# Attention over edges and two norms on one core: all engines' steps in a new order, gathered rows transposed tile by tile, two closing jobs

## The reference

```python
q = (h @ Wq).reshape(n, H, DK); k = (h @ Wk).reshape(n, H, DK); v = (h @ Wv).reshape(n, H, DK)   # H 8, DK 64
e = einsum('ehd,ehd->eh', k[src], q[dst]) / sqrt(DK)
m = segment_max(e, dst, n); ex = exp(e - m[dst]); z = segment_sum(ex, dst, n); attn = ex / z[dst]
a = segment_sum(attn[:, :, None] * v[src], dst, n).reshape(n, DM)
x = _layernorm(h + a @ Wo, ln1_g, ln1_b)
f = relu(x @ W1 + b1) @ W2 + b2                      # 512 -> 64 -> 512
x = _layernorm(x + f, ln2_g, ln2_b)
out = _layernorm(h + x)                              # a last norm, without gain and bias
```

## Time and profile before

| | us |
|---|---|
| median of 3 runs | 683.0 (682.57 to 683.35) |
| span of the profiled execution | 682.0 |
| TensorE busy (matmuls) | 641.5 (94%) |
| TensorE weight loads, beside the matmuls | 483.8 (71%) |
| VectorE busy | 578.0 (85%) |
| ScalarE busy | 528.3 (77%) |
| GpSimd busy | 401.7 (59%) |
| granted TensorE clock, mean | 0.986 |
| HBM traffic over the span | 135 GB/s |

### The profile page before, as it was taken

How to read it: one execution, slowest core, us unless ns; L and a number is a source line. 1 busy time by engine, 2 the same in 40 slices (tenths; PEclk the granted TensorE clock), 3 DMA queues, 4 the chain that set the end, 5 groups by cost and what they waited for, 6 DMA issues and landing times. The chain is left out here.

```text
span 682.0 us, 10864 instructions
## 1 busy us (share of the span) xinstructions
PE 641.5 (94%) x3520; PEld 483.8 (71%) x3520; DVE 578.0 (85%) x1391; ACT 528.3 (77%) x1140; POOL 401.7 (59%) x363
## 2 busy tenths in 40 slices
PE   5999999999999999999999999999999999999950
PEld 2778877777777777777777777777778778675520
DVE  7668769879898898898889889988989898899792
ACT  2525269877888987988798889878878999698881
POOL 7267244867675865756776574864547726735423
PEclk9999999999999999999999999999999999999995
DMA  7844154644643745674474456455554824536452
GB/s 227 220 101 133 44 123 106 173 122 142 148 121 131 159 121 148 167 157 92 146 177 117 113 161 137 105 168 123 127 128 155 184 62 135 139 77 138 131 113 91
DMA packets 37747, 91.44 MB, mean 134 GB/s; under 512 B 8346, under 2 KB 9642, under 8 KB 37690
## 3 DMA queue, kind: packets, MB, share of 16 engines
q0 software_dynamic: 31536, 82.74, 47.6%
q1 hardware_dynamic: 6154, 8.01, 4.3%
HBM read 71.20 MB, written 20.99 MB: 135 GB/s over the span
## 5 line engine op out<-in xcount | busy, mean ns | idle before, releaser
L558 ACT ACTIVATE squares<-rows,nmean 125x512 bf16<-125x512 f32 x200 | 142.3, 713 | 41.5 <-DVE nmean L902 19.8
L412 POOL DMA_INDIRECT x_rows<-in_x_dram,node_idx x40 | 48.2, 1205 | 56.8 <-DVE rows L917 47.3
L416 POOL DMA_INDIRECT out_dram<-rows,node_idx x40 | 46.4, 1160 | 56.4 <-ACT rows L618 47.0
L473 POOL DMA_DIRECT2D x_rows<-in_L_gnn_ln_b_dram x40 | 52.9, 1372 | 31.1 <-DVE rows L821 21.7
L898 DVE SCALAR_TENSOR_TENSOR rows<-pF,rows 125x512 f32<-125x512 f32 x78 | 50.6, 686 | 23.2 <-PE pF L1103 22.5
L963 PE MATMUL pP<-wo_hi,aT_hi 128*125 128x512 f32 x160 | 65.9, 412 | 0.3 <-DVE aT_lo L848 0.3
L963 PE MATMUL pP<-xTs_hi,wv_hi 128*128 128x500 f32 x160 | 65.8, 411 | 0.0
L963 PE MATMUL pP<-xTd_hi,wq_hi 128*128 128x500 f32 x160 | 65.4, 409 | 0.1
L963 PE MATMUL pP<-xTs_hi,wk_hi 128*128 128x500 f32 x160 | 63.5, 397 | 0.6 <-ACT q L539 0.6
L963 PE MATMUL pP<-wo_lo,aT_hi 128*125 128x512 f32 x160 | 63.1, 394 | 0.0
L963 PE MATMUL pP<-wo_hi,aT_lo 128*125 128x512 f32 x160 | 63.0, 394 | 0.0
(11 more groups left out here) (197 smaller groups left out, 1760.6 us busy)
## 6 DMA issues: line engine op xcount, KB each, us to landing
x_rows<-in_L_gnn_ln_b_dram POOLq DMA_DIRECT2D x40, 512.0 KB, 6.7
dst_row<-in_dst_dram SPq DMA_DIRECT2D x9, 250.5 KB
q<-in_L_gnn_Wq_dram SPq DMA_DIRECT2D x1, 1024.0 KB, 5.6
rows<-in_L_gnn_Wk_dram SPq DMA_DIRECT2D x1, 1024.0 KB, 7.8
rows<-in_L_gnn_Wv_dram SPq DMA_DIRECT2D x1, 1024.0 KB, 6.8
x_rows<-in_L_gnn_Wo_dram SPq DMA_DIRECT2D x8, 128.0 KB, 6.0
xd<-in_x_dram,dst_idx POOLq DMA_INDIRECT x40, 4.6
xs<-in_x_dram,src_idx POOLq DMA_INDIRECT x40, 3.8
```

The lines of the kernel that those rows point to most:

```text
L412: pool.indirect_dma_start(rows, None, x, bass.IndirectOffsetOnAxis(ap=table[:, column:column + 1].bitcast(U32), axis=0), bounds_check=N - ...
L416: pool.indirect_dma_start(out, bass.IndirectOffsetOnAxis(ap=table[:, column:column + 1].bitcast(U32), axis=0), rows, None, bounds_check=N ...
L473: pool.dma_start(xr_wide[n], bass.AP(tensor=be2.tensor, offset=be2.offset, ap=[[0, P], [0, 2], [1, D]]), accum_op=ALU.add).then_inc(s[f"be ...
L558: ins = act.activation(squares[:, t, :], w[n][:, t, :], ACT.Square, bias=nmean[c][n][:, t:t + 1], accum_out=sq[c][n][:, t:t + 1])
```

## The change

**New order.** PLAN is replaced by one list per engine with a due number for each step of each round ("-" where a round lacks the step), and `sequence()` only sorts it. Nearly every engine's order is another one. The parts that the steps below speak of:

- TensorE, head. Before: ... COUNT0 COUNT1 TXD0 to TXD3 COUNT2 Q0 Q1 TXS0 TXS1 COUNT3 COUNT4 TXS2 Q2 TXS3 ROFF Q3 K0 FOLD K1 .... After: TURN1 TURN2 OFFS TURNF TXD0 FOLD TXD1 COUNT0 COUNT1 TXD2 TXD3 COUNT2 COUNT3 TXS0 Q0 TXS1 Q1 TXS2 TXS3 COUNT4 Q2 Q3 ROFF TXD0/1 (TXD0 of round 1) BITS K0 to K3 TXD1/1 TXD2/1 V0 S ....
- VectorE, head. After: CAST1 TABD CAST2 FLAG FILLI TABS FILLT DIG LQ CNT0 CNT1 B1 TXD0 TXD1 CNT2 CNT3 TXD2 TXD3 FW LK TXS0 mask TXS1 CNT4 TXS2 TXS3 LV RANK LIST TXD0/1 K0 LO K1 N1.sum N0.sum .... Before, LQ stood behind CNT0 and CNT1, CNT3 and CNT4 behind the last TXD, and RANK and LIST ahead of LV. N1.sum of round 1 stands ahead of H1 of round 0.
- ScalarE, head. After: HQ TXD0 to TXD3 HK TXS0 Q0 TXS1 Q1 TXS2 TXS3 HV Q2 Q3 TXD0/1 HO ....
- GpSimd. Before, GXD/0 GXS/0 BIAS GXD/1 SAVE FI/0 mask/0 GXS/1 GN1/0 GN0/0 FI/1 ..., with FI/2 to FI/9 one in a round. After: INIT GXD/0 GXS/0 GXD/1 mask/0 GXS/1 BIAS GN1/0 SAVE GN0/0 FI/1 FI/0 N0.be/0 N1.be/0 FI/2 GE0/0 GXD/2 FI/3 mask/1 GN1/1 GXS/2 N1.out/0 GE1/0 E0.be/0 N1.be/1 FI/4 FI/6 FI/7 GXD/3 mask/2 E1.be/0 FI/5 GE0/1 E0.out/0 GXS/3 FI/8 FI/9 GE1/1 E1.out/0 E0.be/1 GN0/1 GXD/4 ...: all ten FI stand ahead of GXD/4. INIT is the second half of the constants, now a step of the list.
- Round 8 on TensorE. Before: ... K3/9 N1.T/8 O0/8 N1.F1/8 O1/8 N1.F2/8 S/9 O2/8 O3/8 ... V3/9 N0.F1/8 E1.T/8 N0.F2/8 E1.F1/8 N1.T/9 E1.F2/8 N1.F1/9 O0/9 .... After: the score S/9 stands ahead of N1.F2 of round 8, and behind V3/9 come N0.F2/8 E1.T/8 E1.F1/8 E1.F2/8 N1.T/9 O0/9 N1.F1/9 O1/9 O2/9 N1.F2/9 O3/9.
- Closing. Before: three closing jobs (E0, E1, N0). After: E0.T E0.B9 E0.F19 N0.T E0.F29 E1.B9 N0.F1 E1.T E1.F19 N0.F2 E1.F29 (all of round 9): N0 of round 9 is a regular job with norm, seed and z on ScalarE, and only E0 and E1 close. `banks_before()` names the job that last used the pF banks (E1, the second closing job, uses pP banks and is left out).
- ScalarE around the score of round 9. Before, N1.sq, E0.norm and N0.sd of round 8 stood ahead of it; after, behind. N1.norm and N1.T of round 9 move to places further back.

**Fillers.** 19 are left of 58, all in the head: behind TURN1 6, OFFS 2, TURNF 9, TXD0 2.

**Tables.** CAST is split in CAST1 (dst) and CAST2, TURN in TURN1 (dst) and TURN2; TABD writes the destination table first, TABS the rest; FILLI is split in FILLI and FILLT.

**Gathers tile by tile.** Each of the four gathers has a semaphore of its own and waits for the turn of its own tile; a TX step transposes one tile (four chunks of 125 columns) where it transposed one chunk of four tiles, and ScalarE and VectorE write its result to hi and lo with a stride. FI has a semaphore for each round (filled_0 to filled_9) in place of two.

**Weights.** SyncE issues Wk only when all of xd has landed and Wv only when all of xs has; w2 stands behind Wk, and g_all, bias_all and Wo behind Wv.

```diff
-PERIOD = 7684
-SLOT_PERIOD = {"N0": 7687, "N1": 7689}
...
-FILLERS = {
-    (0, "TURNF"): 8, (0, "COUNT0"): 2, (0, "COUNT1"): 2, (0, "TXD1"): 4, (0, "TXD3"): 3, (0, "COUNT2"): 2, (8,
-    "N0.F2"): 16, (8, "E1.F1"): 4, (8, "E1.F2"): 11, (9, "E0.B9"): 2, (9, "E0.F19"): 4
-}
+FILLERS = {(0, "TURN1"): 6, (0, "OFFS"): 2, (0, "TURNF"): 9, (0, "TXD0"): 2}
...
-            due.append((i * SLOT_PERIOD.get(step.strip("!<>").replace("GN", "N")[:2] if "." in step or "GN" in step else "", PERIOD) + int(times[kind] if len(times) > 1 else times[0]), i, n, step.strip("!<>")))
-    return [(i, step) for _, i, n, step in sorted(due)]
+        due += [(int(t), i, n, step) for i, t in enumerate(times) if t != "-"]
+    return [(i, step) for _, i, _, step in sorted(due)]
...
+        def by_chunk(bank):
+            return bank[:, 0:EG].rearrange("p (k n) -> p k n", k=KC)
...
+        def banks_before(i, slot):
+            earlier = [one for one in jobs[:job[i, slot]] if one != closing[1]]
+            return earlier[-1] if earlier else None
...
             sp.dma_start(stage["q"], Wq.rearrange("(k p) n -> p k n", p=P)).then_inc(s["wq_loaded"], 16)
-            sp.dma_start(stage["k"], Wk.rearrange("(k p) n -> p k n", p=P)).then_inc(s["wk_loaded"], 16)
...
-            on.wait_ge("xd_loaded", 64)
-            sp.dma_start(stage["v"], Wv.rearrange("(k p) n -> p k n", p=P)).then_inc(s["wv_loaded"], 16)
+            for t in range(4):
+                on.wait_ge(f"xd_loaded_{t}", 16)
+            sp.dma_start(stage["k"], Wk.rearrange("(k p) n -> p k n", p=P)).then_inc(s["wk_loaded"], 16)
             for h in range(2):
                 sp.dma_start(w2[DFF * h:DFF * h + DFF, :], W2).then_inc(s["w2_loaded"], 16)
-            on.wait_ge("xs_loaded", 64)
+            for t in range(4):
+                on.wait_ge(f"xs_loaded_{t}", 16)
+            sp.dma_start(stage["v"], Wv.rearrange("(k p) n -> p k n", p=P)).then_inc(s["wv_loaded"], 16)
...
                 elif step == "GXD":
                     on.wait_ge("tables_done", 1)
-                    on.wait_ge("xd_turned", 4 * i)
                     for t in range(4):
-                        gather(xd[:, t, :], dst_idx, 4 * i + t, "xd_loaded")
+                        if i:
+                            on.wait_ge("xd_turned", 4 * i - 3 + t)
+                        gather(xd[:, t, :], dst_idx, 4 * i + t, f"xd_loaded_{t}")
...
-                    on.wait_ge(f"filled_{i % 2}", 64 * (i // 2 + 1))
+                    on.wait_ge(f"filled_{i}", 64)
...
-                    act.activation(hi[:, k, :], pT_of(i, step)[:, 0:EG], ACT.Copy).then_inc(s[f"{which}_hi"], 1)
+                    act.activation(hi[:, :, R * t:R * t + R], by_chunk(pT_of(i, step)), ACT.Copy).then_inc(s[f"{which}_hi"], 1)
...
-                    on.wait_ge(f"{which}_loaded", 64 * (i + 1))
+                    on.wait_ge(f"{which}_loaded_{t}", 16 * (i + 1))
                     bank_free(i, step)
-                    for t in range(4):
-                        ins = pe.transpose(pT_of(i, step)[:, R * t:R * t + R], rows[0:R, t, P * k:P * k + P], ident[0:R, 0:R])
+                    for k in range(KC):
+                        ins = pe.transpose(pT_of(i, step)[:, R * k:R * k + R], rows[0:R, t, P * k:P * k + P], ident[0:R, 0:R])
...
                     elif what == "B9":
-                        before = closing.index((i, slot))
-                        if before == 1:
+                        if (i, slot) == closing[1]:
                             on.wait_ge("hx_done", 4 * ROUNDS)
                         else:
-                            j, old = job_before(i, slot) if before == 0 else closing[0]
+                            j, old = banks_before(i, slot)
...
-                        on.wait_ge("seeded_1", nth("act.F1", slot, i))
+                        on.wait_ge("seeded_1", nth("act.seed", slot, i))
```

More of the change, by code:

```diff
@@ L30 @@
[L30 to L34, removed]
@@ L56 @@
[L56 to L61, removed]
@@ L76 @@
+61670 65393; N0.z 15765 21784 26742 32723 38142 44487 51054 57215 61934 65615; E0.F19 - - - - - - - - - 63173; E1.F19
+- - - - - - - - - 64231
 """,
     "dve": """
-!CAST -263381; !FLAG -243336; !TABS -242836; !FILLI -241863; !FW -55094; !B1 -55229; !LQ -172721; !LK -85485;
-!LV -54432; !LO 76605; !CNT0 -198287; !CNT1 -179760; !CNT2 -159099; !CNT3 -97504; !CNT4 -91086; !RANK -79616;
-!DIG -211902; !LIST -79575; TXD0 -162172 -29587 125840 127315 124482; TXS0 -89151 40059 130890 130776 132032;
-K0 -51732 66249 133633 132533 134452; W0 18249 122663 136307 136222 169476; N0 35421 125323 136834 136488 170118;
@@ new lines @@
+5309 10400 16134 22568 29235 35860 40599 45324 50662; FW 2005; LK 2069; TXS0 2310 6278 11599 18579 24174 30435 36122
+42076 49062 55367; mask 2369 7118 10596 16662 23820 28850 35420 40352 47109 53056; TXS1 2427 6876 11792 18924 24644
+30494 36181 42252 49128 55425; CNT4 2486; TXS2 2730 7060 12502 18983 24703 31932 36946 43585 49659 55985; TXS3 2788
+7894 12561 19590 25303 31990 37005 43644 49718 56051; LV 2847; RANK 3088; LIST 3365; K0 3738 8365 13340 20170 26365
+32465 37874 44390 50159 56504; LO 3963; K1 4204 8637 14562 20442 26685 32812 38238 44603 50797 56871; N1.sum 4263 8044
@@ L118 @@
+N0.m3 15087 21512 25884 32056 37761 43918 50721 56930 61648 65374; N0.r3 15350 21746 26234 32438 37964 44449 50942
+57177 61862 65577; E0.norm9 - - - - - - - - - 62684; E1.norm9 - - - - - - - - - 63653; E1.z9 - - - - - - - - - 65385
 """,
     "pool": """
-!SAVE -5825; !BIAS -40385; GXD -191598 -28838 122318 123741 124346; GXS -100305 39633 129311 131877 129664;
-FI 11329 78418 132148 139332 155267; GN0 71513 141862 142816 141861 224198; GE0 111452 138189 140544 141386 216328;
-GN1 52511 134171 139643 140034 163143; GE1 114908 144515 142071 143811 232509; mask 20690 83236 131262 135698 143659;
@@ new lines @@
+36820 43165 49102; mask 2439 7288 11253 16732 23890 29065 35819 40478 47179 53126; BIAS 3188; GN1 3450 7513 17523
+23106 30271 35033 41203 48494 53921 59082; SAVE 3712; GN0 3802 15046 21472 25876 31964 37657 43689 50622 57018 61546;
+FI 4596 4072 5454 6764 9157 11645 9681 10205 13217 13741; N0.be 5120 17054 23368 27828 34069 39485 46014 53369 58915
+63111; N1.be 5287 8990 19990 26754 32750 39318 43951 50884 56266 61346; GE0 5978 12169 18607 24663 30764 36558 42903
+48835 54907 60285; N1.out 8299 18345 26138 31026 36296 42019 49923 54631 60008 64436; GE1 8561 14265 19655 27183 32917
@@ L290, in graph_attention @@
         pe_steps = sequence("pe")
-        turns = [(i, step, half) for i, step in pe_steps if step[:2] == "TX" or step.endswith((".T", ".T9"))
+        turns = [(i, step, half) for i, step in pe_steps if step[:2] == "TX" or step.endswith(".T")
                  for half in range(1 if step[:2] == "TX" else 2)]
@@ L299, in graph_attention @@
         closing = [(i, step.split(".")[0]) for i, step in pe_steps if step.endswith(".F19")]
-        assert len(closing) == 3 and closing == jobs[-3:]
+        assert len(closing) == 2
         assert all(products[-1] in pe_steps[:pe_steps.index((i, f"{slot}.B9"))] for i, slot in closing[1:])
```

255 lines of the change are left out of this document (141 added, 114 removed).

## The result

The changed kernel takes 718.03 us (median; 712.53 to 719.42) against 683.17 for the kernel before in the same comparison: a ratio of 1.0498, 95% interval 1.0460 to 1.0537. That is 35 us slower, where 680.3 was forecast with a range of 673 to 688. The profiled execution took 719.42 with a span of 717.5.

A forecast was written before the change was run, and what follows sets the result against it. TensorE was taken to bound the stage between the scores, ScalarE round 8, small steps the closing. Terms 2.0 + 0.1 + 0.6 + 0 = 2.7 off 682.0 give 679.3, plus 1.0 around the span: 680.3 us, range 673 to 688.

The forecast's parts named there:

- Head: Up to the first score matmul: 3.3 us gained less 1.3 for late weights, 2.0 won (bounds -0.2 and 3.3).
- term of 1.3: Head, late weights: 0.6 us for TensorE's wait at ROFF and 0.7 for the wait of LO on VectorE.
- GpSimd's queue: Rival, middle: FI steps delay GN1 of round 1, holding VectorE and TensorE; up to 687 us, chance 0.15.
- The point of 90.4: Middle: landing time of GN1 of round 1 at which the 3.7 us counted for the change are gone.
- Middle: First to last score: 1.1 us off as N1.F2 leaves, 1.0 lost to GpSimd's queue; 0.1 won (bounds -7 and 2.3).
- round 8: Last score to the last products: ScalarE busiest, its work nearly even; 0.6 us won (bounds -2 and 3).
- only TensorE's own work counts: Middle: TensorE is busy 536.32 of 537.5 us, so its own work, hardly changed, sets the stage.
- nearly even: Round 8, ScalarE: gives away N1.norm and N1.T of round 9, takes N1.sq, E0.norm and N0.sd of round 8.
- 79% of the span has 1.2 us left to win: Between first and last score: TensorE idles only 1.2 us, whatever the other engines do.
- The prediction's own sign of being wrong: TensorE idling more than 4 us between the scores, or a round's work itself being shorter.
- The clock falls in the holes of round 8: Rival, round 8 without fillers: small matmuls slow down, 2.5 us lost, 682.8 up to 685 us, chance 0.08.
- Closing: Closing jobs at the end: two instead of three, one B9 less on TensorE; 0 us won (bounds -2 and 2).

The follow-up runs named there:

- E0: Not a run: a job of the kernel, one of three closing jobs before the change and one of two after; no time of its own.
- e1: The changed kernel, order untouched, with the eleven square roots between S and XP made as exp(0.5 ln(v)): 688.66 us, ratio 1.0076.
- e4: The changed kernel with FI of rounds 2 to 9 back to one in a round: 716.23 us, ratio 1.0483.
- e7: e1 with FI of rounds 2 to 9 one in a round: 688.03 us, ratio 1.0063.
- e2: The kernel before with ten pairs of table loads added on ScalarE, ahead of XP or LN: 706.83 us, ratio 1.0334.
- e3: The kernel before without its 37 fillers of rounds 8 and 9: 685.92 us, ratio 1.0033.
- e6: e1 plus the 37 fillers that the kernel before has in rounds 8 and 9: 691.00 us, ratio 1.0116.
- e9: The changed kernel, order untouched, with every root as exp(-0.5 ln(v)) on ScalarE and no reciprocals on VectorE: 690.78 us, ratio 1.0106.
- e12: The kernel before with the head of the change alone, weights issued as before: 681.41 us, ratio 0.9973.
- e13: e12 with the weights issued as in the change (Wk once xd has landed, Wv once xs has): 682.45 us, ratio 0.9986.
- e5: The changed kernel with eight of the eleven roots between S and XP moved to just behind XP on ScalarE: 719.96 us, ratio 1.0567.
- e10: The kernel before with every root as exp(-0.5 ln(v)) on ScalarE and no reciprocals on VectorE: 688.61 us, ratio 1.0081.

## Why the prediction was wrong, step by step

**Head: right in sign, under half the size.** The first product came at 20.05 (20.6 forecast), with the three steps ahead of it. On the old order the head gains 0.8 us with the late weights, for which 2.0 was forecast (inside the bounds), and 1.85 with early ones, where the forecast's terms give 3.3. So the late weights cost 1.0 against a term of 1.3. That these are near is luck, as the parts of the term were sized wrong: TensorE didn't wait at ROFF at all, and LO, taken at 0.7, waited 5.19, since wo's eight loads were issued last of all and took 9.9 us to land (6.0 before). VectorE and then the first score:

```profile
44.59 0.69 DVE L660 TENSOR_TENSOR wo_lo<-x_rows,wo_hi 128x512 fp32r<-128x512 f32 x1 [5.19 <-ACT wo_hi L523]
...
53.68 2.00 PE L1058 MATMUL pS<-q,same_head 128*128 128x500 f32 x2 [2.88 <-DVE q L798]
```

The forecast for that score was 51.3; after has 53.7, with matmuls at 1.2 GHz from 16.1 to 22.9 ahead of it, and e1 has 51.9.

**GpSimd's queue: right in its pattern, and beside the point.** GN1 of round 1 was forecast to issue its last gather at 82.7 and land at 86.3. It stood behind the sixteen FI as worked out and was some 2 us later:

```profile
84.97 1.01 POOL L420 DMA_INDIRECT x_rows<-in_x_dram,node_idx  x1 [0.30 <-PE pT L1051]
...
88.48 1.29 DVE L892 BATCH_NORM_STATS2 st<-x_rows 125x6 f32<-125x512 f32 x2 [2.23 <-DMA x_rows<-in_x_dram,node_idx]
```

VectorE waited 2.2 us, and TensorE's idle time up to the next score was 0.34, so the 1.0 that the sum charges for this wait isn't found. The point of 90.4, from which this rival decides, was not reached, and e4 and e7 agree.

**Middle and round 8: wrong.** The step that failed is that ScalarE's new order was priced at nothing: in the middle by leaving it out ("only TensorE's own work counts", with a term for GpSimd's queue alone), in round 8 by the sentence that its exchange of steps around S of round 9 is "nearly even". That sentence counted busy time and not which table a step needs: N1.sq and N0.sd moved from ahead of S to behind it, across the load that stands in the earlier trace rows itself with its 1.28 us. E1.sd of round 8, which neither the list of the change nor the prediction names, moved there from the other side, from behind XP. So it was in seven of the eight rounds from 2 to 9: of the eleven roots four came from ahead of S and seven from behind XP. The sum had 0.1 won for the middle and 0.6 for round 8; the runs show 24.4 and 5.8 us lost, and 29.4 of the whole 34.9 gone without the 21 loads (e1). Two things were at hand: twenty loads in before's groups by line, and the new order of ScalarE. Eleven crossings of two loads each would have been some 28 us. And by the words "79% of the span has 1.2 us left to win" a stage in which TensorE has no slack was read as one that can't lose. In e2 it loses 16.3 us there for 19.8 that ScalarE is busy more. The prediction's own sign of being wrong, more than 4 us of TensorE's idle time between the scores, came with 17.4.

The Trainium skill (ScalarE: Activation LUTs, Table sets: the hidden batching unit) says that activation calls are to be batched by table set. The trace agrees: eleven roots among the calls of Exp and Ln brought 21 loads, 26.9 us. The same page (What ACT_TABLE_LOAD costs) adds 1.38 us of drain to a load of 1.283. The trace does not: the operation ahead of the load ends at 421.44, the load runs from 421.47 to 422.75, and the root starts at 422.76.

**The clock: the rival's fall came, its price is not shown.** "The clock falls in the holes of round 8" was priced at 2.5 us. It does fall there (0.93 in after, 0.90 in e1), and in after at holes of five earlier rounds too, so the forecast that the clock stays at 1.0 to the last matmul failed. e3 measures 2.6, but for the old order and with the six fillers of the closing gone as well; in the new order the time rose when fillers kept the clock up (e6). By the Trainium skill (TensorE: Matmul & The Clock Gate, HAM oscillation) bursts behind pauses start slow. The stretch from 425.7 to 432.5 at a hole of 2.49 us agrees; the matmuls behind the hole at 641.9 don't.

**Closing: right in length** (31.5), but the stretch behind the last matmul grew from 23.9 to 25.4, in e1 too. That 1.5 us and the 4.6 us more idle time that e1 has between the scores than before are the largest parts of the 5.3 us that are left without the loads. FI (e7) and ScalarE's further loads (e9) are ruled out for it; the late weights may have a part (1.0 between e12 and e13). Which steps of the order make the rest stays open.

## What to carry to other kernels

Where an order is rewritten, read each engine's list for state that its instructions share, above all the function table of ScalarE: a step of 0.3 us that crosses a table load brings two or three loads with it. Where one engine is busy 99.8% of a stage, ask how much slack the others' lists have before they hold it up: such a stage has little to win and much to lose. When a change mixes a good part with a bad one, put the good part alone on the old order: here the head alone wins 0.27%, while the whole loses 5%.

## What the runs showed that was not expected

A Ln that follows a root gets a table without Exp, although the table that S loads serves both: the load at L552 (423.08) is followed by one more for Exp at L555 (425.90), with no root between the two. Round 6 is the one round of after where this can be seen; in e5 it comes twice (eight loads for three roots). Without the root neither load is there (e1).

Fillers that hold the clock at 2.4 GHz are worth 2.6 us in one order (e3) and cost 2.3 in another (e6), in the same round.

Twenty loads less and no reciprocals on VectorE did not make the old order faster but 5 us slower (e10), with ScalarE 2.4 us and VectorE 14.5 us less busy. Of the 3.4 us that its profile is longer than before's, 2.2 are there by the first score, ahead of any root; a further 0.8 lie between the scores. So in that run the longer chain at each root can explain the smaller part at most.
